# Attention and feed-forward block in float32 halves: probabilities times values by batch in four matmuls of 256 columns, later copies of the values, an earlier first mixing

## The chip, the cores and the metric

The kernel runs on one core of one Trainium2 chip. The metric is the device time of one execution in microseconds; lower is better. Of the kernel before there are three runs and one profiled execution.

## What is computed

32 batches of 64 tokens of width 1024, one transformer block. Cut to what matters:

```python
W = weights[condition]                                  # one 64x64 of 16, by batch
xm = einsum('bct,bcd->bdt', x, W)                       # the mixing: within a batch, over its 64 tokens
q, k, v = heads of xm @ Wq.T, xm @ Wk.T, xm @ Wv.T      # 32 query heads, 8 key heads, head width 128
q, k = rmsnorm(q) * q_norm_w, rmsnorm(k) * k_norm_w
attn = softmax(q @ k.T / sqrt(128) + bias)              # alibi slopes and causal mask, 64 x 64 by batch and head
x = x + (attn @ v) @ Wo.T
base = x @ weight.T + bias + scale * ((x @ a_sel.T) @ b_sel.T)        # a low-rank adapter, by batch
x = x + base @ W_base.T + b_base + 0.5 * (sum over 3 experts of irfft of decoded encodings)
```

All of it is float32. The feed-forward weights are folded into one matrix on the chip first.

## The kernel before

**Precision.** Every float32 operand of a matmul is kept as two halves that TensorE reads at full pace: hi, a copy rounded by ScalarE (`copy`, line 1226), and lo, what is left of it, a subtraction on VectorE (`low`, line 1480). A product of two such operands is three matmuls: hi by hi, hi by lo, lo by hi (`products`, line 1019). Weights come by DMA into four raw buffers (SyncE's queue), and w_hi and w_lo make a chunk in a ring of six slots.

**Order.** The whole order of the program is written out by a planner class, `Order`. Time in it is counted in quarters: a quarter is the products of one chunk, six matmuls of 512 columns. Each engine executes its own stages in the order of one common list, and waits for semaphores of the others. The table AT gives the due time of each stage in quarters after the products of its step; LATE is added for the last query step of a block; a stage is put at the first quarter that reaches its due time.

**Blocks.** Four blocks of 512 tokens, each of four tiles of 128 tokens, so two batches per tile. A block has key-value units (kv) and query units (q), each of four steps, one per tile; output units (o and p), which multiply the heads with Wo by a scheme of seven products; and two feed-forward units (f). In a block the order is kv, q, q, kv, o, q, q, kv, o, q, q, kv, o, q, q, p, o, f, f.

**A query step.** Four quarters of products give 128 tokens by 4 heads in one of four main banks. Then: square (ScalarE), mean (VectorE), rstd (GpSimd), scale (VectorE, which also empties the bank), query_t (TensorE transposes, line 1180), q_hi and q_lo, score (lines 1196 and 1197), alibied, biased and peak (VectorE), exp (ScalarE, line 1385), total, inverse and prob (VectorE), prob_t (TensorE transposes, line 1204), p_hi (ScalarE, line 1395), p_lo (VectorE, line 1681), pv (TensorE, line 1215), heads (ScalarE). A kv step has the same norm for its two key heads, gain (VectorE), key_t, k_hi, k_lo, and copies its two value heads as v_hi (ScalarE, straight after the products) and v_lo (VectorE).

**The product with the values.** Values have the tokens of both batches of a tile on the partitions. pt_hi and pt_lo hold the transposed probabilities of batch 0 in rows 0 to 63 of their first 256 columns and those of batch 1 in rows 64 to 127 of the other 256; the rest is zero from the start. So three matmuls of 512 columns give both batches:

```python
for m, (a, p) in enumerate(((v_hi, pt_hi), (v_hi, pt_lo), (v_lo, pt_hi))):
    mm = eng.matmul(pv_bank[...], a[:, t, g % 2, :], p[...], start=m == 0, stop=m == 2)
```

**Setup and the first mixing.** The setup folds the feed-forward weights: product(n, u) for n = 0 to 8 and u = 0, 1 is 24 matmuls (5.4 us) each; n = 8 stands for the adapter's b. Results leave by f_copy (ScalarE) and f_store (GpSimd's queue) through acc, so that x2 and x3, which load tiles 2 and 3 of x into the same place, wait for all f_store. A mixing of a tile is split_mix (x_hi, x_lo) and mix: four banks, each with four matmuls (lines 1103 and 1105), a_hi (ScalarE), a_rest and a_lo (VectorE, lines 1480 and 1483). `prepare(both=True)` loads and splits one weight chunk. "Rounds" (sums_load, sums_add t1 to t4, sums_store) form sums of parts of Wo on VectorE and GpSimd's queue; their due times are ROUND_AT.

**biased_x** (GpSimd, line 1848) adds a bias to a tile of acc, which VectorE's acc of unit f waits for. It is emitted with each tile's transposes of x1 (`transpose_x1`), which wait for the earlier tile's a_lo in the same banks.

Of the kernel before, what the change touches and what calls it, by code (L numbers as in the profile page):

```python
# [16 lines left out]
P = 128  # L17
# [25 lines left out]
AT = dict(square=0.15, mean=1.3, scale=1.7,  # L43
          tq=2.8, tq_hi=3.4, tq_lo=3.9,
          s=4.8, s_add=5.5, s_exp=6.3, s_norm=6.4,
          tp=7.9, tp_hi=8, tp_lo=8.6,
          v=10, v_hi=10.7, v_lo=11.3,
# [5 lines left out]
LATE = dict(s=0.5, s_add=0.5, s_exp=0.5, s_norm=0.5, tp=1.1, tp_hi=1.1, tp_lo=1.1, v=2.1, v_hi=2.1)  # L53
# [28 lines left out]
ROUND_AT = (0.5, 17, 33.5, 104, 180)  # L82
# [105 lines left out]
class Order(Plan):  # L188
# [34 lines left out]
    def setup(self):  # L223
# [55 lines left out]
        for n in range(KT):  # L279
# [17 lines left out]
            if n == 6:  # L297
                self.sums_load(*ROUNDS[2])
            self.product(n, 1)
# [138 lines left out]
    def blocks(self):  # L438
# [74 lines left out]
    def kv_step(self, k):  # L513
        self.wide(k, ("scale", (k,)))
        self.tick()
        base = self.quarter
        self.add("v_hi", k)

        def after_scale():
            self.add("gain", k)  # L520
            self.at(base, AT["tq"], transpose)
# [5 lines left out]
        self.norm(k, lambda: self.add("v_lo", k), after_scale)  # L527

    def norm(self, k, after_mean, after_scale):
# [3 lines left out]
        def mean():  # L533
            self.add("mean", k)
            self.add("rstd", k)
            after_mean()
# [4 lines left out]
        self.later(AT["square"], lambda: self.add("square", k))  # L541
# [3 lines left out]
    def q_step(self, k, g, t):  # L545
# [32 lines left out]
        def transpose_p():  # L578
            self.fill("pt", "prob_t", (k,), "p_lo")
            self.at(base, when("tp_hi"), lambda: self.add("p_hi", k))  # L580
            self.at(base, when("tp_lo"), lambda: self.add("p_lo", k))
# [13 lines left out]
        self.norm(k, lambda: None, after_scale)  # L595
# [58 lines left out]
    def transpose_x1(self, blk, t):  # L654
# [4 lines left out]
        self.add("biased_x", blk, t)  # L659
# [46 lines left out]
def build_program(nc, d, out):  # L706
# [3 lines left out]
    with ctx:  # L710
# [35 lines left out]
        v_hi = sb("v_hi", [P, TILES, 2, HD], F32R)  # L746
        v_lo = sb("v_lo", [P, TILES, 2, HD], F32R)
# [6 lines left out]
        prob = sb("prob", [P, 256])  # L754

# [45 lines left out]
        enc_rows = [v_hi[:, :, :, :].rearrange("p a b n -> p (a b n)"), v_lo[:, :, :, :].rearrange("p a b n -> p (a b n)")]  # L801
# [95 lines left out]
        def tile_of(k):  # L897
            return step(k)[3]
# [1053 lines left out]
```

## Time and profile before

| | |
|---|---|
| median of 3 runs | 2399.7 us (2398.89 to 2400.05) |
| the profiled execution | 2400.53 us, its span 2398.7 us |
| TensorE busy | 2368.9 us (99%), 11578 matmuls |
| VectorE busy | 1750.3 us (73%) |
| ScalarE busy | 1330.4 us (55%) |
| GpSimd busy | 280.5 us (12%) |
| matmuls of probabilities and values | 3 x 128, of 512 columns |

The span runs from the first to the last instruction; the execution's own time has some 2 us around it. Matmuls are pipelined, so that the time from one's start to the next's start counts, not its duration.

### The profile page before, as it was taken

To read this page: it belongs to the slowest core of one execution; us is meant where nothing else is said; L and a number is where in the kernel's file an instruction comes from. 1 tells how busy PE (TensorE), PEld (TensorE's weight loads), DVE (VectorE), ACT (ScalarE), POOL (GpSimd) and SP (SyncE) were. 2 spreads that over 40 slices of the span, in tenths; PEclk is the share of its full clock that TensorE was granted. 3 is DMA by queue.
4 is the path that set the end of the run, shared out by engine and by line. 5 is a ranking of instruction groups with operands and counts; after the bars stand their busy time and mean duration, and the time that the engine had idled before them with its cause. 6 is when DMAs were issued, how large, how long until landed. Compare 5 with 4: busy or idle time off the path is not lost.

```text
span 2398.7 us, 32788 instructions
## 1 busy us (share of the span) xinstructions
PE 2368.9 (99%) x11578; PEld 1967.4 (82%) x11578; DVE 1750.3 (73%) x2866; ACT 1330.4 (55%) x3305; POOL 280.5 (12%) x336
## 2 busy tenths in 40 slices
PE   8989999999999999999999999999999999999998
PEld 6878888888888888888888888888888888888886
DVE  6768878686847867777856777777876686868682
ACT  4246656566625656566724656565744565657560
POOL 0222010101111001010011101010011101010110
PEclk9999999999999999999999999999999999999999
DMA  7765434441542242423343242423244242424250
GB/s 258 257 256 199 154 134 148 140 149 63 188 145 92 88 139 76 141 79 129 134 156 118 71 158 71 158 71 123 97 170 148 77 147 69 153 77 141 70 194 35
DMA packets 88436, 316.12 MB, mean 132 GB/s; under 512 B 12716, under 2 KB 13228, under 8 KB 87124
## 3 DMA queue, kind: packets, MB, share of 16 engines
q1 hardware_dynamic: 70292, 247.14, 30.5%
q0 software_dynamic: 16256, 62.92, 7.2%
q10 hardware_dynamic: 1728, 3.98, 0.5%
q8 instruction: 94, 1.54, 0.3%
q14 instruction: 66, 0.54, 0.1%
HBM read 282.54 MB, written 31.46 MB: 131 GB/s over the span
## 4 chain that ended last, share of the span: by engine, by line
PE 94%; DVE 4%; issue 1%; DMA 1%; ACT 0%; POOL 0%; ACTq 0%; POOLq 0%; DVEq 0%
PE main L1019 79%; PE pv_bank L1215 4%; PE qt_bank L1180 3%; PE s_bank L1196 2%; PE s_bank L1197 2%; PE pt_bank L1204 1%; PE pt_bank L1019 1%; DVE ring L1480 1%; DVE act_lo L1480 0%; DVE act_lo L1483 0%; DVE setup L1480 0%; PE qt_bank L1117 0%; PE s_bank L1117 0%; DMA mask<-in_masks 0%; DMA t_scratch<-sums 0%
## 5 line engine op out<-in xcount | busy, mean ns | idle before, releaser
L1019 PE MATMUL main<-ring,act_hi 128*128 128x512 f32 x3584 | 1149.2, 402 | 0.1
L1019 PEld LDWEIGHTS main<-ring,act_hi 128*128 128x128 f32 x3584 | 641.3, 189 | 112.7 <-issue 2.1
L1019 PE MATMUL main<-ring,act_lo 128*128 128x512 f32 x1792 | 702.5, 392 | 0.0
L1019 PE MATMUL main<-ring,lefts 128*128 128x512 f32 x2688 | 624.3, 391 | 0.0
L1480 DVE TENSOR_TENSOR ring<-raw,ring 128x1024 fp32r<-128x1024 f32 x448 | 554.4, 1240 | 59.5 <-ACT ring L1226 58.0
L1019 PEld LDWEIGHTS main<-ring,lefts 128*128 128x128 f32 x2688 | 501.7, 188 | 103.0
L1226 ACT ACTIVATE ring<-raw 128x1024 fp32r<-128x1024 f32 x448 | 472.5, 1057 | 180.8 <-PE main L1019 163.6
L1019 PEld LDWEIGHTS main<-ring,act_lo 128*128 128x128 f32 x1792 | 336.8, 188 | 74.6
L1816 POOL TENSOR_TENSOR rstd<-mean,half 128x4 f32<-128x4 f32 (+1 forms) x192 | 174.7, 910 | 1568.5 <-DVE mean L1605 1568.3
L1385 ACT ACTIVATE prob<-score,peak 128x64 f32<-128x64 f32 x512 | 136.7, 338 | 157.3 <-DVE peak L1660 156.8
L1357 ACT ACTIVATE sq<-main 128x128 f32<-128x128 f32 x640 | 168.8, 277 | 70.7 <-PE main L1019 68.4
L1483 DVE TENSOR_TENSOR acc<-main,acc 128x512 f32<-128x512 f32 x164 | 112.2, 685 | 88.7 <-PE main L1019 88.4
L1681 DVE TENSOR_TENSOR pt_lo<-pt_bank,pt_hi 64x256 fp32r<-64x256 f32 x256 | 107.9, 421 | 72.8 <-ACT pt_hi L1395 71.1
L1395 ACT ACTIVATE pt_hi<-pt_bank 64x256 fp32r<-64x256 f32 x256 | 97.0, 379 | 112.4 <-PE pt_bank L1204 110.6
L1480 DVE TENSOR_TENSOR lefts<-quads,lefts 128x1024 fp32r<-128x1024 f32 x112 | 136.7, 1220 | 9.8 <-ACT lefts L1226 7.7
L1622 DVE TENSOR_TENSOR qn<-main,rstd 128x512 f32<-128x512 f32 (+1 forms) x192 | 114.3, 596 | 36.7 <-POOL rstd L1816 36.7
L1226 ACT ACTIVATE qt_hi<-qt_bank 128x512 fp32r<-128x512 f32 x128 | 76.7, 599 | 107.3 <-PE qt_bank L1180 102.3
L1226 ACT ACTIVATE lefts<-quads 128x1024 fp32r<-128x1024 f32 x112 | 118.7, 1060 | 29.9 <-PE main L1019 27.8
L1480 DVE TENSOR_TENSOR qt_lo<-qt_bank,qt_hi 128x512 fp32r<-128x512 f32 x128 | 87.9, 687 | 64.7 <-ACT qt_hi L1226 64.7
L1357 ACT ACTIVATION_READ_ACCUMULATOR sq<-main 128x1 f32 x640 | 132.8, 207 | 0.0
L1197 PE MATMUL s_bank<-k_t,qt_lo 128*128 128x64 f32 x512 | 117.2, 245 | 0.0
L1196 PE MATMUL s_bank<-k_t,qt_hi 128*128 128x128 f32 x512 | 114.6, 285 | 0.2
(172 smaller groups left out, 2390.4 us busy)
## 6 DMA issues: line engine op xcount, KB each, us to landing
raw<-in_wq SPq DMA_DIRECT2D x128, 512.0 KB, 4.0
raw<-t_scratch SPq DMA_DIRECT2D x128, 512.0 KB, 3.3
raw<-in_wo SPq DMA_DIRECT2D x96, 512.0 KB, 3.3
raw<-in_wkv SPq DMA_DIRECT2D x64, 512.0 KB, 4.1
sums<-in_wo POOLq DMA_DIRECT2D x32, 512.0 KB, 6.6
t_scratch<-sums POOLq DMA_DIRECT2D x32, 512.0 KB, 4.2
raw<-f_scratch SPq DMA_DIRECT2D x32, 512.0 KB, 5.5
acc<-in_x POOLq DMA_DIRECT2D x16, 512.0 KB, 3.7
```

Of the source, the lines that this page charges most:

```text
L1019: mm = eng.matmul(bank, a, b, start=start and n == 0 and m == 0, stop=stop and n == len(terms) - 1 and m == 2, skip_group_check=further)
L1196: eng.matmul(s_bank[:, a:a + 2 * SEQ], lh, keys, start=True, stop=False)
L1197: mm = eng.matmul(s_bank[:, a:a + SEQ], ll, keys[:, 0:SEQ], start=False, stop=True)
L1226: eng.activation(dst, src, ACT.Copy).then_inc(done[stage], 1)
L1357: act = eng.activation(sq[:, tile(h)], norm_bank(k)[:, tile(h)], ACT.Square, accum_out=ssum[:, h:h + 1])
L1385: act = eng.activation(prob[:, cols], score[:, cols], ACT.Exp, bias=peak[:, r:r + 1], scale=-1.0)
L1395: act = eng.activation(pt_hi[rows_of(b), b, :], pt_bank[rows_of(b), 0:256], ACT.Copy)
L1480: eng.tensor_tensor(dst, src, f32(upper), ALU.subtract).then_inc(done[stage], 1)
L1483: eng.tensor_tensor(dst, a, b, ALU.add).then_inc(done[stage], 1)
L1622: eng.tensor_tensor(heads_of(norm_tile(k)[:, cols], heads), heads_of(norm_bank(k)[:, cols], heads), along(rstd[:, 0:heads], heads), ALU.mu ...
L1681: rest = eng.tensor_tensor(pt_lo[rows_of(b), b, :], pt_bank[rows_of(b), 0:256], f32(pt_hi[rows_of(b), b, :]), ALU.subtract)
L1816: eng.tensor_tensor(rstd[:, 0:heads], mean[:, 0:heads], half[:, 0:heads], ALU.pow).then_inc(done[stage], 1)
```

## The change

1. The values of a tile are kept by batch: `values[:, t, g, b, :]` has v_hi of batch b in the batch's own half of the partitions and v_lo of the same batch in the other half. pt_hi has the hi probabilities of a batch in both halves: a new stage p_twice (ScalarE) copies each from one half into the other. One matmul with `values` and pt_hi so gives v_hi by p_hi plus v_lo by p_hi, and one with pt_lo gives v_hi by p_lo: two matmuls of 256 columns for each batch.
2. v_hi is two copies of 64 rows, and waits for scale (due at 1.9 instead of straight after the products); v_lo is two subtractions that write the other half (due 2.3, behind gain).
3. Due times: p_twice 9.2, pv 10.6 (10 before), heads 11.5 (10.7); LATE 1.2 and 1.6 (1.1 and 2.1).
4. The first mixing: tiles 0 and 1 are mixed before product(7, 1) and product(8, 0); x_hi and x_lo of tile 2 stand before product(8, 0); tile 2 is mixed after chunk 4; tile 3 is split before the first kv step and mixed before the second.
5. The rounds of the sums come 2 to 4 quarters later.
6. biased_x is emitted for two tiles together, and waits for the later one's a_lo.

```diff
-          tp=7.9, tp_hi=8, tp_lo=8.6,
-          v=10, v_hi=10.7, v_lo=11.3,
+          tp=7.9, tp_hi=8, tp_again=9.2, tp_lo=8.6,
+          v=10.6, v_hi=11.5,
...
-ROUND_AT = (0.5, 17, 33.5, 104, 180)
+ROUND_AT = (4.5, 20, 35.5, 104, 180)
...
+            if n == KT - 1:
+                self.mix(0, 0)
             self.product(n, 1)
...
+        self.mix(0, 1)
+        self.split_mix(0, 2)
         self.product(KT, 0)
+        for i in range(UNIT_CHUNKS):
+            self.prepare(both=True)
+        self.product(KT, 1)
         self.prepare(both=True)
-        self.mix(0, 0)
+        self.mix(0, 2)
         self.prepare(both=True)
-        self.prepare(both=True)
-        self.split_mix(0, 2)
-        self.prepare(both=True)
+        self.split_mix(0, 3)
         self.load(("lora_a",), ("loraa_lo", ()))
         self.add("loraa_hi")
         self.add("loraa_lo")
-        self.product(KT, 1)
-        self.mix(0, 1)
-        self.prepare(both=True)
-        self.prepare(both=True)
         self.add("fx_store")
...
-            if k == 0:
-                self.split_mix(0, 3)
-            if k in (1, 2):
-                self.mix(0, k + 1)
+            if k == 1:
+                self.mix(0, 3)
...
-        self.add("biased_x", blk, t)
+        if t % 2 == 1:
+            for half in (t - 1, t):
+                self.add("biased_x", blk, half)
...
-        v_hi = sb("v_hi", [P, TILES, 2, HD], F32R)
-        v_lo = sb("v_lo", [P, TILES, 2, HD], F32R)
+        values = sb("values", [P, TILES, 2, BPT, HD], F32R)
...
-                    w.wait_ge("p_hi", k)
+                    w.wait_ge("p_twice", k)
...
-                    for m, (a, p) in enumerate(((v_hi, pt_hi), (v_hi, pt_lo), (v_lo, pt_hi))):
-                        mm = eng.matmul(pv_bank[:, :, :].rearrange("p b n -> p (b n)"), a[:, t, g % 2, :],
-                                        p[:, :, :].rearrange("p b n -> p (b n)"), start=m == 0, stop=m == 2)
+                    for b in range(BPT):
+                        both = values[:, t, g % 2, b, :]
+                        eng.matmul(pv_bank[:, b, :], both, pt_hi[:, b, :], start=True, stop=False)
+                        mm = eng.matmul(pv_bank[:, b, :], both, pt_lo[:, b, :], start=False, stop=True)
...
+                elif stage == "p_twice":
+                    k, = key
+                    w.wait_ge("p_hi", k)
+                    for b in range(BPT):
+                        act = eng.activation(pt_hi[rows_of(1 - b), b, :], f32(pt_hi[rows_of(b), b, :]), ACT.Copy)
+                    act.then_inc(done["p_twice"], 1)
...
                 elif stage == "v_lo":
                     k, = key
                     w.wait_ge("square", k)
-                    low(v_lo[:, tile_of(k), :, :], norm_bank(k)[:, 2 * HD:4 * HD].rearrange("p (j n) -> p j n", j=2),
-                        v_hi[:, tile_of(k), :, :], stage, k)
+                    w.wait_ge("v_hi", k)
+                    for b in range(BPT):
+                        rest = eng.tensor_tensor(values[rows_of(1 - b), tile_of(k), :, b, :], values_in(k, b),
+                                                 f32(values[rows_of(b), tile_of(k), :, b, :]), ALU.subtract)
+                    rest.then_inc(done[stage], 1)
```

How this moves the stages, at three places. The first is TensorE's list at the product of probabilities and values in a query unit (qt_bank is the transposes of the queries, main a quarter of products). Before:

```order
L1215 MATMUL pv_bank<-pt_hi,v_hi 128x512
L1215 MATMUL pv_bank<-pt_lo,v_hi 128x512
L1215 MATMUL pv_bank<-pt_hi,v_lo 128x512
L1019 MATMUL main<-ring,act_hi 128x512 x2
L1019 MATMUL main<-ring,act_lo 128x512
L1019 MATMUL main<-ring,act_hi 128x512 x2
L1019 MATMUL main<-ring,act_lo 128x512
L1180 MATMUL qt_bank<-ident,qn_75 128x128 x4
```

Now:

```order
L1027 MATMUL main<-ring,act_hi 128x512 x2
L1027 MATMUL main<-ring,act_lo 128x512
L1027 MATMUL main<-ring,act_hi 128x512 x2
L1027 MATMUL main<-ring,act_lo 128x512
L1224 MATMUL pv_bank<-pt_hi,values 128x256
L1225 MATMUL pv_bank<-pt_lo,values 128x256
L1224 MATMUL pv_bank<-pt_hi,values 128x256
L1225 MATMUL pv_bank<-pt_lo,values 128x256
L1188 MATMUL qt_bank<-ident,qn_75 128x128 x4
```

The product stands one quarter later, directly ahead of the query transposes.

The second place is ScalarE's list where a query unit's last softmax meets the first step of a kv unit (v_hi and now values are the copies of the values, sq the squares, prob the exp of the last query step). Before:

```order
L1395 ACTIVATE pt_hi<-pt_bank 64x256 x2
L1226 ACTIVATE v_hi<-main 128x256
L1357 ACTIVATE sq,ssum<-main 128x128 x2
L1385 ACTIVATE prob<-score,peak 128x64 x4
L1226 ACTIVATE quads<-pv_bank 128x2x4x64
```

Now:

```order
L1406 ACTIVATE pt_hi<-pt_bank 64x256 x2
L1368 ACTIVATE sq,ssum<-main 128x128 x2
L1412 ACTIVATE pt_hi<-pt_hi 64x256 x2
L1360 ACTIVATE values<-main 64x2x128 x2
L1396 ACTIVATE prob<-score,peak 128x64 x4
```

The copies of the values, which now wait for VectorE's scale, stand directly ahead of the exp.

The third place is VectorE's list at the end of the setup, (ring is w_lo of a chunk, act_lo a piece of a mixing, x_odd x_lo of tile 3, lefts x_lo of tile 2, extra the adapter's parts). Before:

```order
L1483 TENSOR_TENSOR act_lo<-pv_bank,act_lo 128x2x128
L1480 TENSOR_TENSOR ring<-raw_69,ring 128x1024
L1480 TENSOR_TENSOR ring<-raw_70,ring 128x1024
L1480 TENSOR_TENSOR x_odd<-acc,x_odd 128x1024
L1480 TENSOR_TENSOR act_lo<-qt_bank,act_hi 128x2x128
```

Now:

```order
L1497 TENSOR_TENSOR ring<-raw_68,ring 128x1024
L1497 TENSOR_TENSOR act_lo<-qt_bank,act_hi 128x2x128
L1500 TENSOR_TENSOR act_lo<-qt_bank,act_lo 128x2x128
L1497 TENSOR_TENSOR act_lo<-s_bank,act_hi 128x2x128
L1500 TENSOR_TENSOR act_lo<-s_bank,act_lo 128x2x128
L1497 TENSOR_TENSOR act_lo<-pt_bank,act_hi 128x2x128
L1500 TENSOR_TENSOR act_lo<-pt_bank,act_lo 128x2x128
L1497 TENSOR_TENSOR act_lo<-pv_bank,act_hi 128x2x128
L1500 TENSOR_TENSOR act_lo<-pv_bank,act_lo 128x2x128
L1497 TENSOR_TENSOR ring<-raw_69,ring 128x1024
L1497 TENSOR_TENSOR x_odd<-acc,x_odd 128x1024
L1497 TENSOR_TENSOR extra<-raw_70,extra 128x1024
```

The split of tile 3 stands behind both w_lo and the mixing of tile 2 as before, but TensorE's mixing of tile 3, which needs it, has moved from the third kv step to the second.

## Rows read from the trace of the kernel before

**Rows 1.** The page: busy us (share of the span) x instructions, by engine.

```profile
PE 2368.9 (99%) x11578; PEld 1967.4 (82%) x11578; DVE 1750.3 (73%) x2866; ACT 1330.4 (55%) x3305; POOL 280.5 (12%) x336
```

**Rows 2.** The page: the chain that ended last, by engine.

```profile
PE 94%; DVE 4%; issue 1%; DMA 1%; ACT 0%; POOL 0%; ACTq 0%; POOLq 0%; DVEq 0%
```

**Rows 3.** Waits of TensorE: engine line <- releaser: us, times, longest.

```profile
PE qt_bank L1180 <- DVE qn L1629: 5.3, 3, 3.5
...
PE qt_bank L1117 <- DVE act_lo L1480: 2.4, 1, 2.4
PE qt_bank L1103 <- DVE act_lo L1483: 1.9, 2, 1.0
```

**Rows 4.** Behind the longest wait: busy PE, PEld, DVE, ACT, POOL; PEclk.

```profile
155.00:159.00 4.00, 3.63 (x12) 3.06 (x13) 1.87 (x3) 0.77 (x2) 0.00 (x0) 0.57 0.05 19
```

**Rows 5.** Chain in order of time, block 1: start, us, what.

```profile
881.78 0.22 PE pt_bank L1204 x2
...
885.65 0.68 PE pv_bank L1215 x3
886.34 1.36 PE main L1019 x6
```

**Rows 6.** The same view after the wait of 2.4 us.

```profile
660.33 6.41 PE main L1019 x21
```

**Rows 7.** Low-rank stage: the chain, then line 1019's loads, min/median/max.

```profile
666.74 2.87 PE pt_bank L1019 x24
...
L1019 PEld LDWEIGHTS pt_bank<-act_hi,extra x16: 187/192/192, 649.8 to 652.7; 128*128 128x128 f32 x16
```

**Rows 8.** ScalarE in order of time, one query step.

```profile
224.85 0.77 ACT L1395 ACTIVATE pt_hi<-pt_bank 64x256 fp32r<-64x256 f32 x2 [1.01 <-PE pt_bank L1204]
...
226.66 1.07 ACT L1226 ACTIVATE ring<-raw 128x1024 fp32r<-128x1024 f32 x1
```

**Rows 9.** From query to key steps: ScalarE, VectorE, TensorE in order of time.

```profile
244.52 1.07 ACT L1385 ACTIVATE prob<-score,peak 128x64 f32<-128x64 f32 x4 [1.93 <-DVE peak L1660]
...
244.40 0.41 DVE L1622 TENSOR_TENSOR qn<-main,rstd 128x256 f32<-128x256 f32 x1
...
246.29 0.43 DVE L1675 TENSOR_TENSOR prob<-prob,inv 128x256 f32<-128x256 f32 x1
...
248.02 0.38 PE L1204 MATMUL pt_bank<-ident,prob 128*128 128x128 f32 x2
```

**Rows 10.** All engines at 654 us in order of time.

```profile
654.06 2.68 POOL L1848 TENSOR_TENSOR acc<-acc,bias_eff 128x1024 f32<-128x1024 f32 x1 [4.07 <-PE s_bank L1117]
...
654.39 3.43 DVE L1480 TENSOR_TENSOR ring<-raw,ring 128x1024 fp32r<-128x1024 f32 x1
```

**Rows 11.** DMA issues at 125.25 and from 138: count, KB, us to landing.

```profile
acc<-in_x POOLq DMA_DIRECT2D x1, 512.0 KB, 7.4
...
raw<-in_wq SPq DMA_DIRECT2D x2, 512.0 KB, 5.9
```

**Rows 12.** VectorE in order of time at the first mixing.

```profile
143.12 0.69 DVE L1480 TENSOR_TENSOR extra<-main,extra 128x512 fp32r<-128x512 f32 x1
143.72 0.42 DVE L1480 TENSOR_TENSOR act_lo<-qt_bank,act_hi 128x256 fp32r<-128x256 f32 x1
...
149.14 1.22 DVE L1480 TENSOR_TENSOR x_odd<-acc,x_odd 128x1024 fp32r<-128x1024 f32 x1
```

**Rows 13.** TensorE at the end of product 8.

```profile
133.78 0.39 PE L1019 MATMUL main<-setup,act_lo 128*128 128x512 f32 x1
```

**Rows 14.** TensorE in the mixing of tile 3.

```profile
159.03 0.33 PE L1103 MATMUL s_bank<-mixw,x_odd 128*128 128x256 f32 x1
159.20 0.22 PE L1105 MATMUL s_bank<-mixw,x_odd 128*128 128x128 f32 x1
159.25 0.34 PE L1103 MATMUL s_bank<-mixw,x_odd 128*128 128x256 f32 x1
...
160.41 0.45 PE L1019 MATMUL main<-ring,act_hi 128*128 128x512 f32 x1
```

More of the change, by code:

```diff
@@ L40 @@
 SCALING = 16.0 / 32.0
-AT = dict(square=0.15, mean=1.3, scale=1.7,
+AT = dict(square=0.15, mean=1.3, scale=1.7, values=1.9, values_lo=2.3,
           tq=2.8, tq_hi=3.4, tq_lo=3.9,
           s=4.8, s_add=5.5, s_exp=6.3, s_norm=6.4,
-          tp=7.9, tp_hi=8, tp_lo=8.6,
-          v=10, v_hi=10.7, v_lo=11.3,
+          tp=7.9, tp_hi=8, tp_again=9.2, tp_lo=8.6,
+          v=10.6, v_hi=11.5,
           add=1.6,
@@ L51 @@
           w_hi=0.3, w_lo=0.9)
-LATE = dict(s=0.5, s_add=0.5, s_exp=0.5, s_norm=0.5, tp=1.1, tp_hi=1.1, tp_lo=1.1, v=2.1, v_hi=2.1)
+LATE = dict(s=0.5, s_add=0.5, s_exp=0.5, s_norm=0.5, tp=1.2, tp_hi=1.2, tp_again=1.2, tp_lo=1.2, v=1.6, v_hi=1.6)
 OPS = (("11", "11", "a"), ("s3", "t3", "d"), ("12", "21", "a"), ("s2", "t2", "b"),
@@ L513, in kv_step @@
     def kv_step(self, k):
-        self.wide(k, ("scale", (k,)))
+        self.wide(k, ("v_lo", (k,)))
         self.tick()
         base = self.quarter
-        self.add("v_hi", k)
+        self.later(AT["square"], lambda: self.add("square", k))
         def after_scale():
             self.add("gain", k)
+            self.at(base, AT["values"], lambda: self.add("v_hi", k))
+            self.at(base, AT["values_lo"], lambda: self.add("v_lo", k))
             self.at(base, AT["tq"], transpose)
@@ L526, in transpose, with norm @@
             self.at(base, AT["tq_lo"], lambda: self.add("k_lo", k))
-        self.norm(k, lambda: self.add("v_lo", k), after_scale)
-    def norm(self, k, after_mean, after_scale):
+        self.norm(k, after_scale)
+    def norm(self, k, after_scale):
         self.norm_no[k] = len(self.norms)
@@ L535, in mean @@
             self.add("rstd", k)
-            after_mean()
         def scale():
@@ L580, in transpose_p @@
             self.at(base, when("tp_hi"), lambda: self.add("p_hi", k))
+            self.at(base, when("tp_again"), lambda: self.add("p_twice", k))
             self.at(base, when("tp_lo"), lambda: self.add("p_lo", k))
@@ L594, in after_scale @@
                 self.at(base, when(name), work)
-        self.norm(k, lambda: None, after_scale)
+        self.later(AT["square"], lambda: self.add("square", k))
+        self.norm(k, after_scale)
     def o_step(self, k, blk, pair, m):
@@ L799, in build_program @@
         bias_parts = k_flat.rearrange("p (u s n) -> p u s n", u=2, s=2)
-        enc_rows = [v_hi[:, :, :, :].rearrange("p a b n -> p (a b n)"), v_lo[:, :, :, :].rearrange("p a b n -> p (a b n)")]
-        enc_hi = v_hi[0:ENC, :, :, :].rearrange("p a b n -> p (a b n)")
-        enc_lo = v_lo[0:ENC, :, :, :].rearrange("p a b n -> p (a b n)")
+        v_flat = values[:, :, :, :, :].rearrange("p t g b n -> p (t g b n)")
+        enc_rows = [v_flat[:, 0:CHUNK], v_flat[:, CHUNK:2 * CHUNK]]
+        enc_hi, enc_lo = (part[0:ENC, :] for part in enc_rows)
         x_even = [lefts[:, 2, i, :, :, :].rearrange("p a h n -> p (a h n)") for i in range(2)]
@@ L1344, in _ @@
                     k, = key
-                    w.wait_ge("mm", k, 3)
+                    w.wait_ge("scale", k)
                     if last_heads(k) is not None:
@@ L1349, in _ @@
                         w.wait_ge("weff_mm", KT, 1, 3)
-                    copy(v_hi[:, tile_of(k), :, :], norm_bank(k)[:, 2 * HD:4 * HD].rearrange("p (j n) -> p j n", j=2), "v_hi")
+                    for b in range(BPT):
+                        act = eng.activation(values[rows_of(b), tile_of(k), :, b, :], values_in(k, b), ACT.Copy)
+                    act.then_inc(done["v_hi"], 1)
                 elif stage == "square":
@@ L1608, in _ @@
                     w.wait_ge("square", k)
-                    low(v_lo[:, tile_of(k), :, :], norm_bank(k)[:, 2 * HD:4 * HD].rearrange("p (j n) -> p j n", j=2),
-                        v_hi[:, tile_of(k), :, :], stage, k)
+                    w.wait_ge("v_hi", k)
+                    for b in range(BPT):
+                        rest = eng.tensor_tensor(values[rows_of(1 - b), tile_of(k), :, b, :], values_in(k, b),
+                                                 f32(values[rows_of(b), tile_of(k), :, b, :]), ALU.subtract)
+                    rest.then_inc(done[stage], 1)
                 elif stage == "scale":
```

5 lines of the change are left out of this document (3 added, 2 removed).

## The prediction

> **What bounds the kernel now.** Read the busy shares first: TensorE is busy for 2368.9 us, 99% of the span, VectorE for 73%, ScalarE for 55%, GpSimd for 12% [rows 1]. The chain that ended last is 94% TensorE and 4% VectorE [rows 2]. So the kernel's time is its list of matmuls at their pace, plus a few stalls: a cut in the matmuls is worth its full time, work added to the other engines is worth nothing while TensorE waits for none of it. The waits of TensorE are next [rows 3]: outside the start and the setup's beginning they are 5.3 us for transposes of keys and queries that wait for VectorE's gain (3.5 in one piece), 1.9 for mixing banks, 2.4 for the transposes of x1. A long wait has a tail: after the one of 3.5 us the granted clock of the next 4 us is 0.57 of full, which is the lower level, 1.2 GHz, for most of it [rows 4]; after the one of 2.4 us, 21 matmuls that take 4.8 us elsewhere (0.227 each, by six in 1.36) take 6.41 [rows 5, 6]. A wait over 2 us thus costs some 1.6 us on top.
>
> **Part 1, the products of probabilities and values.** There are 128 (one for each query step). Each is now three matmuls of 512 columns, 0.68 us from its first to the next stage's first [rows 5]. Afterwards it is four of 256. The trace has matmuls of this very shape (128x128 stationary, 256 moving columns, each with its own weight load) in the low-rank stage: 24 in 2.87 us, 0.1196 each [rows 7]. Four are 0.478 us, so one step saves 0.20 us, and 128 save **25.8 us**. Both ends: if columns alone counted, a matmul of half the columns would take half of 0.227, four of them 0.454, a saving of 29 us. The other end is weight loads that don't hide: one lasts 0.187 to 0.192 [rows 7], four are 0.76 us, a loss of 0.08 a step, 10 us in all. I take the 0.1196, since it is the same instruction with the same weight load.
> The Trainium skill (TensorE: Matmul & The Clock Gate, Back-to-back issue gap) gives N/2.4 + 2.5 ns between matmuls at the full clock: 216 ns for 512 columns, 109 for 256. By it, called an estimate, the group would go from 0.65 to 0.44 us and the 128 would save 27 us. The rows show 227 and 120, some 10 ns more each, and I go by them.
>
> **Part 2, what the four matmuls need.** pt_hi must hold each batch's probabilities in both halves of the partitions, so ScalarE gets two more copies a step (p_twice), 64x256 from SBUF to SBUF. The nearest row is p_hi, two of 64x256 from PSUM in 0.77 us [rows 8]; a copy from SBUF of four times the columns takes 1.07. I take 0.8 us a step, 102 us in all. v_hi becomes two copies of 0.38 for one of 0.384 (64 steps, +24 us). ScalarE goes from 55% to about 61%. VectorE's v_lo becomes two of 0.42 for one (+27 us of 1750). None of it lies on TensorE's list; it costs only where the cover is gone. The cover: now the transposes of the probabilities end at 882.0 and the product starts at 885.65, 3.6 us later [rows 5]. The product's due time goes from 10 to 10.6, which by the order is one quarter (six matmuls, 1.36 us) later, so the window is 5.0 us. In it ScalarE has p_hi (0.77), the next square and, in the worst steps, a ring copy (1.07), all done 2.9 us after p_hi's start [rows 8], then p_twice: 3.7. Over 1 us is left. The exp of the next step, which waits for VectorE, stands behind p_twice. So I cost it at 0.
> v_hi is moved behind scale, and is so ahead of exp where a query unit's last softmax meets the first step of the next key unit (three times a block, 12 in all). There scale ends at 244.82, two copies take 0.76, exp then starts at 245.6 instead of 244.52, and VectorE's total, inverse and prob end at about 247.8 instead of 246.72, with the transposes due at 248.02 less the 0.2 us that the product gives back [rows 9]. The margin of 1.3 us shrinks to about nothing: 0 to 0.3 us each, 12 times; I take **+1 us**. The main bank of a key step is held until v_lo instead of scale, about 1 us of the 16 or more quarters before its next use: nothing.
>
> **Part 3, biased_x.** In block 0 the addition of the bias on GpSimd (2.68 us from 654.06) covers VectorE's w_lo, which lasts 3.43 us instead of 1.24 [rows 10]; behind it on VectorE's queue stand acc and the act_lo that the next transposes of x1 wait for. This is the wait of 2.4 us [rows 3], with 1.6 us of half clock behind it [rows 6]. Now biased_x runs after both tiles' act_lo, so nothing of it runs at 654: w_lo ends 2.2 us earlier and the stall and its tail go, all but 0.2: **-3.8 us**. What it collides with next: two additions back to back (4.9 us) after the second pair, against a w_lo whose chunk is for a later unit, and VectorE has nothing due there. The other three blocks have no such wait, and stay.
>
> **Part 4, the first mixing.** Mixing of tiles 0 and 1 goes ahead, into the products with w2, where VectorE is idle. That takes sixteen pieces of 0.42 off VectorE's queue there, and its two waits (1.9 us) go. But follow the rest. The mixing of tile 0 (1.8 us) stands ahead of the product whose store x2's load waits for, so that x2 and x3 are issued 1.6 us later; x2's load, issued at 125.25, takes 7.4 us [rows 11] and will land at 134.3. On ScalarE x_hi of tile 2 now stands ahead of all six weight copies: it ends at 135.4, x_lo at 136.6, beff_lo 0.7 and w_lo of chunk 0 (1.24) bring 138.5. Chunk 4 is loaded into the buffer that this frees: 5.9 us as the two loads issued there now [rows 11], 144.4. On ScalarE its copy stands ahead of the mixing pieces of tile 2 (1.06, 145.5); on VectorE w_lo (146.7), eight act_lo of 0.42 (150.0), w_lo of chunk 5 (151.3), x_lo of tile 3 (152.5) [rows 12]. TensorE ends product 8 at 133.9 today [rows 13] and 1.8 later now, at 135.8, waits 0.8 for x_lo of tile 2, mixes it, does key step 0, and is at the mixing of tile 3 at 144.0, which needs that last x_lo: **a wait of 8.5 us**, in place of those of 0.8 (mixing), 3.5 (keys) and others. Then mixing, key step 1 and 1.6 us of low clock end at 161.6; today the same work ends at 160.4 [rows 14]. So +1.2 us there. After that, today's small waits for keys and queries (1.1, 0.6, 0.3 and less) partly go, as gain stands ahead of v_lo, and the sums' rounds, 2 to 4 quarters later, bring one or two others: 0. I take **+1 us**. Bounds: all of the 9 us of waits and low clock there go (5.3, 1.9 and 1.6), -9; the rounds' collisions come on top, +7.
>
> **Sum.** -25.8 + 1 - 3.8 + 1 = -27.6 us against the profiled execution's 2400.5 us, 2372.9; the median of the runs is 0.8 below that execution, so 2372.
>
> **Rivals.**
> A: the product doesn't get the pace of the low-rank stage. In the mixing, a matmul of 256 columns starts 0.17 us before the next one [rows 14], and at four times 0.17 the new product costs the old 0.68. Against it: there the next is one of 128 columns that starts 0.05 later, and the pair takes 0.23, 0.115 each. If weight loads don't hide at all the product takes 0.76, +10 us, and the whole comes to 2400.5 + 10 + 1 - 3.8 + 1 = 2409, slower than before; it decides from 0.17 us a matmul. Chance 3%.
> B: ScalarE is late with p_twice. From 0.2 us of wait a product the saving is gone, from 0.25 (for example 1.3 us more queue than counted, at each step) the kernel is slower. The order speaks against it; in one step of five it would give 26 waits of some 0.3 us, 2380. With the 12 places of part 2 at 0.3 and a second one like them, 2382. Chance 10%.
> C: part 4 goes as its cover suggests: x2 lands earlier since fewer transfers compete, the wait at tile 3 is 0 to 3 us and has no tail: -6 to -9 instead of +1, 2363. For it: the loads of those 20 us differ among themselves, 7.4 and 5.9 us for the same size [rows 11], so the queue before them counts for much. Chance 15%.
> D: the edit does nothing that shows. Excluded but for A: 512 columns fewer a step stand in the order.
>
> **How the numbers follow.** My own case, parts 1 to 4 as summed, has 72%, and its own range is 2366 to 2380: 3 us for part 1's pace (112 to 125 ns), 4 for part 4. With B and C the range is 2362 to 2383. 0.2% is 4.8 us, about what a measurement of this kernel can tell from no change. Faster by more than that: all of my case, B and C but for a tail, 0.94. Within it 0.03 (B at its worst, A at 0.165). Slower 0.03 (A).
>
> **What would show it.** Right: four matmuls of the product at some 0.12 us from start to start; TensorE's busy time down by some 26 us; no waits of TensorE for pt_hi; no w_lo of over 3 us near 654; TensorE's longest wait the mixing of tile 3 near 144, 8 us, with a low clock behind it. Wrong: starts 0.17 apart (A); waits on pv_bank for ScalarE (B); the mixing of tile 3 without a wait (C); several waits of the probabilities' transposes for VectorE at the changes from query to key units (part 2).

## The result, and the profile after

| | before | after |
|---|---|---|
| median | 2399.88 us (4 runs, 2398.89 to 2400.09) | 2434.95 us (4 runs, 2433.82 to 2436.59) |
| ratio | | 1.0144, 95% interval 1.0132 to 1.0156 |
| span of the profiled execution | 2398.7 us | 2433.0 us |

The changed kernel is 35 us slower. The forecast was 28 us faster, 2372 in a range of 2362 to 2383: wrong, in sign too.

The page of the changed kernel, its busy shares and its chain, which answer to [rows 1, 2]:

```profile
PE 2365.7 (97%) x11706; PEld 1970.9 (81%) x11706; DVE 1784.7 (73%) x2930; ACT 1464.8 (60%) x3625; POOL 296.4 (12%) x336
...
PE 84%; DVE 9%; issue 2%; ACT 1%; DMA 1%; POOL 1%; DVEq 0%; ACTq 0%; POOLq 0%
```

TensorE's busy time is only 3 us less than before, and the span is 34 us longer: TensorE waits more, and works part of the time at the lower clock, where a matmul counts as busy for longer. VectorE's share of the chain has gone from 4% to 9%. What TensorE waits for is in the waits of the changed kernel, against [rows 3] (what waited, for what, us in total, times, the longest):

```profile
PE qt_bank L1188 <- DVE qn L1649: 30.3, 25, 2.2
PE qt_bank L1111 <- DVE x_odd L1497: 9.4, 1, 9.4
PE pv_bank L1058 <- ACT pt_lo L1266: 4.6, 1, 4.6
PE qt_bank L1188 <- DVE qn L1642: 3.5, 3, 1.9
PE s_bank L1204 <- issue: 1.9, 4, 1.1
```

The second row is the mixing of tile 3, which part 4 put at 8.5 us. The first is what the forecast missed: transposes of keys (L1188) that wait for gain (L1649), 30.3 us in 25 places, where it was 5.3 in 3.

**An account by places.** Both kernels do the same 192 transposes of keys and queries in the same order. The start of each after the change, less its start before, is a running difference; where it steps, time is lost or won. From the two traces:

| place | us |
|---|---|
| the start, up to the first key step behind query units (246.42 before, 255.41 after) | +9.0 |
| transposes of the fourth key step of a unit with an o unit behind it: 12 places, 2.12 each | +25.4 |
| transposes of the second and third: 12 places, 0.25 and 0.28 | +6.4 |
| the o unit behind the fourth: 8 of the 12 places, 1.6 each | +12.9 |
| end of block 0, start of block 1 | -4.2 |
| starts of blocks 1 to 3 | +1.2 |
| all else: the products, less small waits | -16.2 |
| **sum, at the last transpose** | **+34.5** |

Three rows, 44.7 us, belong to one pattern. The timeline of the kernel before at the first of the twelve places, VectorE from the third key step's transposes (258.96) to the fourth's (264.72), with GpSimd's rstd between its rows (start, duration, engine, line, operation; in brackets the idle time before it):

```profile
257.77 1.22 DVE L1480 TENSOR_TENSOR ring<-raw,ring 128x1024 fp32r<-128x1024 f32 x1
258.90 1.22 DVE L1480 TENSOR_TENSOR lefts<-quads,lefts 128x1024 fp32r<-128x1024 f32 x1
260.04 0.41 DVE L1480 TENSOR_TENSOR k_t<-qt_bank,k_t 128x256 fp32r<-128x256 f32 x1
260.37 1.21 DVE L1480 TENSOR_TENSOR ring<-raw,ring 128x1024 fp32r<-128x1024 f32 x1
261.70 0.17 DVE L1605 TENSOR_SCALAR mean<-ssum 128x2 f32<-128x2 f32 x1
261.78 0.42 DVE L1480 TENSOR_TENSOR v_lo<-main,v_hi 128x256 fp32r<-128x256 f32 x1
...
261.95 0.70 POOL L1816 TENSOR_TENSOR rstd<-mean,half 128x2 f32<-128x2 f32 x1 [5.02 <-DVE mean L1605]
...
262.65 1.23 DVE L1480 TENSOR_TENSOR ring<-raw,ring 128x1024 fp32r<-128x1024 f32 x1 [0.45 <-ACT ring L1226]
263.79 0.42 DVE L1622 TENSOR_TENSOR qn<-main,rstd 128x256 f32<-128x256 f32 x1
264.24 0.42 DVE L1629 TENSOR_TENSOR qn<-qn,kgain 128x256 f32<-128x256 f32 x1
```

The same of the changed kernel, from the third's transposes (268.46) to the fourth's:

```profile
268.78 0.86 DVE L1628 TENSOR_TENSOR values<-main,values 64x256 fp32r<-64x256 f32 x2 [0.38 <-ACT values L1360]
269.67 1.22 DVE L1497 TENSOR_TENSOR ring<-raw,ring 128x1024 fp32r<-128x1024 f32 x1
270.81 1.22 DVE L1497 TENSOR_TENSOR lefts<-quads,lefts 128x1024 fp32r<-128x1024 f32 x1
272.06 0.42 DVE L1497 TENSOR_TENSOR k_t<-qt_bank,k_t 128x256 fp32r<-128x256 f32 x1
272.40 1.22 DVE L1497 TENSOR_TENSOR ring<-raw,ring 128x1024 fp32r<-128x1024 f32 x1
273.53 0.16 DVE L1622 TENSOR_SCALAR mean<-ssum 128x2 f32<-128x2 f32 x1
273.60 1.22 DVE L1497 TENSOR_TENSOR ring<-raw,ring 128x1024 fp32r<-128x1024 f32 x1
...
273.77 1.60 POOL L1836 TENSOR_TENSOR rstd<-mean,half 128x2 f32<-128x2 f32 x1 [6.29 <-DVE mean L1622]
...
275.41 0.42 DVE L1642 TENSOR_TENSOR qn<-main,rstd 128x256 f32<-128x256 f32 x1 [0.59 <-POOL rstd L1836]
...
275.87 0.42 DVE L1649 TENSOR_TENSOR qn<-qn,kgain 128x256 f32<-128x256 f32 x1
...
276.35 0.44 PE L1188 MATMUL qt_bank<-ident,qn 128*128 128x128 f32 x2 [1.96 <-DVE qn L1649]
```

Before, v_lo stands between mean and scale, beside GpSimd's rstd, for which VectorE has to wait anyway: it is free. Now v_lo is two instructions behind gain, and waits 0.38 for v_hi, which starts only when scale has ended. That is 0.38 + 0.86 = 1.24 us more on VectorE's queue between gain and the next mean, at each key step, and here VectorE has the subtractions of ring, lefts, k_t and ring without a break. Mean of the fourth key step starts 2.74 us behind the third's transposes before (261.70 - 258.96) and 5.07 now (273.53 - 268.46): 2.33 more, of which 1.24 comes from this step and the rest from the step ahead of it, which used up a slack of 1.1 us (gain ended at 257.85 before, for transposes at 258.96). From mean to scale it takes 2.09 before and 1.88 now, 0.21 less. 2.33 - 0.21 = 2.12, the step in the table.

In 8 of the 12 places the o unit behind it works at the lower clock for most of 4 us. The changed kernel by stretches behind the second stall (401.9), and behind the first (276.4), which is one of the four places without (us, then busy time and count of PE, PEld, DVE, ACT and POOL, then the granted clock, where 0.50 is 1.2 GHz throughout, the DMA share and GB/s):

```profile
276.40:278.40 2.00, 2.00 (x10) 1.69 (x11) 1.69 (x3) 1.98 (x5) 0.00 (x0) 1.00 0.82 262
401.90:403.90 2.00, 1.91 (x6) 1.63 (x7) 1.58 (x4) 1.98 (x4) 0.00 (x0) 0.58 0.81 256
403.90:405.90 2.00, 2.00 (x6) 1.50 (x6) 1.97 (x3) 0.96 (x2) 0.00 (x0) 0.56 0.11 43
```

**The product itself** did what part 1 said. In the timeline of a query step of the changed kernel:

```profile
334.09 0.28 PE L1224 MATMUL pv_bank<-pt_hi,values 128*128 128x256 f32 x1
334.20 0.28 PE L1225 MATMUL pv_bank<-pt_lo,values 128*128 128x256 f32 x1
334.32 0.28 PE L1224 MATMUL pv_bank<-pt_hi,values 128*128 128x256 f32 x1
334.44 0.29 PE L1225 MATMUL pv_bank<-pt_lo,values 128*128 128x256 f32 x1
334.56 0.60 PE L1188 MATMUL qt_bank<-ident,qn 128*128 128x128 f32 x4
```

Four matmuls in 0.47 us (median of all 128 is 0.475), where three took 0.68 [rows 5].

### The profile page after: what moved, and what is told of

Its sections match the earlier page's. It is cut to its first block, busy times and chain, and to the rows that moved or that the text cites. A ratio compares the mean times of both kernels' runs of the same rounds, so it can differ in the third digit from the quotient of the medians.

```text
span 2433.0 us, 33487 instructions
## 1 busy us (share of the span) xinstructions
PE 2365.7 (97%) x11706; PEld 1970.9 (81%) x11706; DVE 1784.7 (73%) x2930; ACT 1464.8 (60%) x3625; POOL 296.4 (12%) x336
## 4 chain that ended last, share of the span: by engine, by line
PE 84%; DVE 9%; issue 2%; ACT 1%; DMA 1%; POOL 1%; DVEq 0%; ACTq 0%; POOLq 0%
PE main L1027 71%; PE qt_bank L1188 3%; PE s_bank L1204 3%; PE s_bank L1205 2%; DVE ring L1497 1%; DVE lefts L1497 1%; POOL rstd L1836 1%; PE pt_bank L1212 1%; PE pv_bank L1225 1%; PE pv_bank L1224 1%; PE pt_bank L1027 1%; DVE qn L1642 1%; DVE quads L1708 1%; ACT values L1360 1%; DMA acc<-in_x 1%
## 5 line engine op out<-in xcount | busy, mean ns | idle before, releaser
L1027 PE MATMUL main<-ring,lefts 128*128 128x512 f32 x2688 | 637.3, 396 | 0.0
L1027 PEld LDWEIGHTS main<-ring,lefts 128*128 128x128 f32 x2688 | 509.9, 191 | 105.7
L1836 POOL TENSOR_TENSOR rstd<-mean,half 128x4 f32<-128x4 f32 (+1 forms) x192 | 185.5, 966 | 1584.0 <-DVE mean L1622 1579.0
L1188 PE MATMUL qt_bank<-ident,qn 128*128 128x128 f32 x640 | 105.4, 279 | 35.2 <-DVE qn L1649 30.3
L1188 PEld LDWEIGHTS qt_bank<-ident,qn 128*128 128x128 f32 x640 | 73.6, 140 | 58.9 <-DVE qn L1649 44.7
```

The costliest lines, as they stand in the source:

```text
L1027: mm = eng.matmul(bank, a, b, start=start and n == 0 and m == 0, stop=stop and n == len(terms) - 1 and m == 2, skip_group_check=further)
L1188: mm = eng.transpose(qt_bank[:, tile(h)], norm_tile(k)[:, tile(h)], ident[:, :])
L1836: eng.tensor_tensor(rstd[:, 0:heads], mean[:, 0:heads], half[:, 0:heads], ALU.pow).then_inc(done[stage], 1)
```

## The experiments

Theories. **1:** v_lo has left the shadow of rstd; VectorE's queue makes the key transposes late. **2:** ScalarE's added load (p_twice, doubled copies) does. **3:** the first mixing and the rounds shifted the whole stream. Every ratio is to the kernel before, run beside it on the same chip.

### Values early again

```
-        self.wide(k, ("v_lo", (k,)))
+        self.wide(k, ("scale", (k,)))
+        self.add("v_hi", k)
...
-            self.at(base, AT["values"], lambda: self.add("v_hi", k))
-            self.at(base, AT["values_lo"], lambda: self.add("v_lo", k))
...
             self.add("mean", k)
             self.add("rstd", k)
+            after_mean()
```

> The changed kernel with the values copied early again: v_hi (two copies) right behind the key step's products and ahead of its square, v_lo (two) between mean and scale, the main bank given back at scale; the four matmuls of 256 columns, p_twice, biased_x and the first mixing stay as changed. Theory 1 (VectorE's queue): where v_lo stood between mean and scale it lay beside GpSimd's rstd (0.70 us) and cost VectorE's queue nothing; behind gain it adds its own 0.86 us and a wait of 0.38 for v_hi to every key step, mean of the fourth key step before an o unit comes 1.9 us late, and a ring subtraction beside rstd makes that last 1.60 instead of 0.70. By it the 12 places of 2.12 + 0.25 + 0.28 us and the 8 tails of 1.6 us of low clock go, 44.7 us: 2390, between 2383 and 2396. Theory 2 (ScalarE's load): p_twice's 103 us are in the way; then nothing goes: 2430 to 2440. Theory 3 (the first mixing and the rounds moved the whole stream): 2430 to 2440 too.

Measured: 2406.0, ratio 1.0025 (1.0016 to 1.0035). 29 us come back: theory 1 has the cause, its number was too good by 16. The tails (the stretches of low clock) are gone, and the fourth transposes wait 0.68 instead of 1.96, yet they still wait, and the starts of blocks 1 to 3 cost some 4.5 us more than in the changed kernel. The timeline at the first of the twelve places shows why: v_lo is now two instructions, and a ring subtraction still follows it, ahead of scale.

```profile
268.14 0.17 DVE L1622 TENSOR_SCALAR mean<-ssum 128x2 f32<-128x2 f32 x1
268.34 0.86 DVE L1628 TENSOR_TENSOR values<-main,values 64x256 fp32r<-64x256 f32 x2
...
268.39 0.70 POOL L1836 TENSOR_TENSOR rstd<-mean,half 128x2 f32<-128x2 f32 x1 [5.01 <-DVE mean L1622]
...
269.23 1.23 DVE L1497 TENSOR_TENSOR ring<-raw,ring 128x1024 fp32r<-128x1024 f32 x1
270.49 0.42 DVE L1642 TENSOR_TENSOR qn<-main,rstd 128x256 f32<-128x256 f32 x1
```

Mean to scale is 2.35 us against 2.09, and mean itself is 0.52 later behind the third transposes than before (the doubled v_hi stands ahead of square on ScalarE): together 0.78 a place.

### The move of the values alone, on the kernel before

```
-        self.wide(k, ("scale", (k,)))
+        self.wide(k, ("v_lo", (k,)))
...
+            self.at(base, AT["values"], lambda: self.add("v_hi", k))
+            self.at(base, AT["values_lo"], lambda: self.add("v_lo", k))
```

> The kernel before with one part of the change alone: v_hi (one copy of 0.39 us) behind scale and v_lo (one of 0.42) behind it, in the places the change gives them, the bank given back at v_lo; three matmuls of 512 columns, no p_twice, mixing and biased_x as before. Theory 1: VectorE's queue gets 0.39 + 0.42 = 0.8 us per key step instead of 1.24, but the ring subtraction stands beside rstd all the same: 12 stalls of 0.8 to 2.1 us, some with 1.6 us behind them: 2412 to 2440, likeliest 2425. Theories 2 and 3: the same as before, 2400 within 3 us.

Measured: 2409.3, ratio 1.0037 (1.0023 to 1.0052): 9 us slower, with three matmuls and without p_twice. The likeliest value of theory 1 was 16 too high, and the measurement is just outside its range; theories 2 and 3 fall as sole causes. The waits of the key transposes for gain, 5.3 us in 3 places before, are

```profile
PE qt_bank L1181 <- DVE qn L1631: 10.8, 15, 2.1
```

The 12 places are there, at 0.70 us each with no tail, and in each of them rstd lasts 1.60, at the first of them:

```profile
264.35 1.60 POOL L1818 TENSOR_TENSOR rstd<-mean,half 128x2 f32<-128x2 f32 x1 [5.22 <-DVE mean L1606]
```

The 0.8 us that the move adds to VectorE's queue behind the second key step is covered by the slack of 1.1, so that the third's transposes are not late, and only what the third step adds shows at the fourth. So the move alone costs 0.70 a place, and the doubling alone (the kernel with early values above) 0.78 at the fourth step and 0.26 at the second. Both together cost 2.12, 0.25 and 0.28, and mostly a tail. That is more than their sum, since the slack can be used only once.

### The first mixing and rounds as before, and the rounds alone

```
-ROUND_AT = (4.5, 20, 35.5, 104, 180)
+ROUND_AT = (0.5, 17, 33.5, 104, 180)
```

The first of these two kernels has this line and the old order of the mixing of tiles 0 to 3 (mix(0, 0) and mix(0, 1) behind the products of n = 8, and so on as before the change); the second has this line alone.

> The changed kernel with the first mixing and the rounds' places (ROUND_AT) of the kernel before. Theories 1 and 2: only the start changes: the wait of 9.4 us goes and those of 3.5, 1.9 and 1.1 us and a tail of 1.6 come back: 2424 to 2433. Theory 3: the regular stalls go too: 2375 to 2400.

> The changed kernel with the rounds' places (ROUND_AT) of the kernel before, the first mixing as changed. In the changed kernel GpSimd's rstd of the first query step stands behind four loads of the sums' next round, each of which waits for a store to land (185.2 to 188.2), and the query transposes come 1.9 us late, with low clock behind. Theory R (the rounds' places cost most of the 7.4 us at the start): 2428 to 2431. Theory M (the mixing's place costs them): 2433 to 2436.

Measured: 2427.7, ratio 1.0115 (1.0099 to 1.0132), with both; 2428.1, ratio 1.0124 (1.0108 to 1.0139), with the rounds alone. The regular stalls stay in both (here with the rounds alone), so theory 3 falls for them:

```profile
PE qt_bank L1188 <- DVE qn L1649: 29.2, 26, 2.0
```

Both medians are 7 us below the changed kernel's, inside what was expected (theory R for the rounds alone). But the intervals of the ratios meet the changed kernel's, 1.0132 to 1.0156, so the places in the traces have to decide. The first key step behind query units starts at 255.41 in the changed kernel, 249.73 with the old rounds and 247.90 with both. So 5.7 of the 9.0 us at the start are the rounds' places, and 1.8 are the mixing's new place, which the two medians can't tell from nothing. These shares are not a sum: early values alone shorten the start too.

One mechanism of the rounds shows in GpSimd's timeline of the changed kernel:

```profile
185.20 0.53 POOL L1849 DMA_DIRECT2D sums<-in_wo  x1 [2.56 <-DMA t_scratch<-sums]
187.70 0.53 POOL L1849 DMA_DIRECT2D sums<-in_wo  x1 [1.97 <-DMA t_scratch<-sums]
188.25 1.04 POOL L1836 TENSOR_TENSOR rstd<-mean,half 128x4 f32<-128x4 f32 x1
```

The loads of the next round wait on GpSimd's queue until a store has landed, and rstd of the first query step, whose mean was there since 185.46, stands behind them.

### Scale and gain of key steps in mean's quarter

The changed kernel with kv_scale at 1.35, where scale is at 1.7:

```
-        self.later(AT["scale"], scale)
+        self.later(AT["kv_scale" if self.units[self.steps[k][0]][0] == "kv" else "scale"], scale)
```

> The changed kernel with scale and gain of key steps due in the same quarter as mean, so that the ring subtraction (and in some places the three of the softmax) stands behind gain instead of between mean and scale; values stay late. Theory 1: rstd lasts 0.70 in the 12 places instead of 1.60 and scale doesn't wait for 1.22 us of subtraction, so the stall shrinks from 1.96 us to about 1 and has no tail: 2435 - 12 x 0.9 - 13 = 2411, between 2403 and 2420. If the queue and the overlap with rstd are not what holds the key transposes: 2430 to 2440.

Measured: 2411.8, ratio 1.0045 (1.0028 to 1.0062), on the number. At the first place:

```profile
271.66 0.16 DVE L1622 TENSOR_SCALAR mean<-ssum 128x2 f32<-128x2 f32 x1
...
271.90 0.70 POOL L1836 TENSOR_TENSOR rstd<-mean,half 128x2 f32<-128x2 f32 x1 [6.29 <-DVE mean L1622]
...
272.63 0.42 DVE L1642 TENSOR_TENSOR qn<-main,rstd 128x256 f32<-128x256 f32 x1 [0.81 <-POOL rstd L1836]
```

Mean to scale is 0.97 instead of 1.88, which is the whole of the 0.90 us that each of the 12 places gives back; the eight tails go too. Mean is as late as in the changed kernel (5.08 behind the third transposes), so the late mean and the long way from mean to scale are separate terms.

### Without p_twice, and with single copies

Both start from the kernel with early values.

```
-            self.at(base, when("tp_again"), lambda: self.add("p_twice", k))
```

> The changed kernel with early values, less p_twice: ScalarE's two further copies of the probabilities are left out, so the product of their rounded part with the values' remainder is not computed. Theory 1 (VectorE's queue holds the key transposes, ScalarE's added load does not): the same as with early values and p_twice, 2406, between 2402 and 2407. Theory 2 (ScalarE's load counts: v_hi, square and with them mean come later behind p_twice): the waits of 0.7 and 0.4 us at the key transposes that are left shrink by half or more, 2392 to 2400.

Measured: 2403.1, ratio 1.0011 (1.0002 to 1.0021), 2.9 us less than with p_twice. ScalarE's busy time goes from 1466.3 to 1358.2 us, and the waits of key transposes for gain stay:

```profile
PE qt_bank L1187 <- DVE qn L1648: 16.7, 28, 1.9
```

They were 16.8 in 28 with p_twice. Theory 2 falls; 108 us of work on ScalarE cost some 3. The intervals of the two kernels just overlap (this one's ends at 1.0021, the other's begins at 1.0016), but the traces agree with the medians: the first key transposes of block 3 start at 1845.71 here and at 1848.83 with p_twice.

```
-                    for b in range(BPT):
-                        act = eng.activation(values[rows_of(b), tile_of(k), :, b, :], values_in(k, b), ACT.Copy)
+                    act = eng.activation(values[:, tile_of(k), :, 0, :], full, ACT.Copy)
```

and v_lo likewise.

> The changed kernel with early values, v_hi and v_lo each done as one instruction over 128 partitions instead of two over 64: the four matmuls of the product, p_twice and all else run as they are, but the values' parts don't stand where the product needs them, so the products are not the reference's. Theory 1: one 128-partition instruction lasts as long as one over 64 (0.39 and 0.42 us), so the path from products to key transposes is 0.38 shorter, VectorE's queue 0.43; the 12 places of 0.78 + 0.27 and the 3 further ones at the starts of blocks go: 2406 - 12.6 - 2 = 2391, between 2387 and 2397. Theory 2 (p_twice delays them): 2400 to 2406.

Measured: 2388.6, ratio 0.9949 (0.9932 to 0.9966): theory 1, 2 us beyond its likeliest. The waits for gain are down from 16.8 us in 28 places to 4.3 in 13, and at the 12 places there is none:

```profile
PE qt_bank L1188 <- DVE qn L1649: 4.3, 13, 1.0
```

The doubling of v_hi and v_lo accounts for the 12 places that early values had left, and more: 17 us.

### biased_x in its old place

```
-        if t % 2 == 1:
-            for half in (t - 1, t):
-                self.add("biased_x", blk, half)
+        self.add("biased_x", blk, t)
```

> The changed kernel with biased_x in its old place (an addition behind each tile's transposes). If part 3 was right, block 0 gets back its ring subtraction of over 3 us beside GpSimd's addition near 665 and the wait of 2.4 us with its tail: 2435 + 3.8 = 2439, between 2437 and 2441. If the pair of additions costs as much elsewhere (in blocks 1 to 3 of the changed kernel a ring subtraction of 3.4 us begins beside the first of a pair): 2433 to 2436.

Measured: 2438.9, ratio 1.0163 (1.0146 to 1.018). The median is 3.9 us over the changed kernel's, but these four runs lie between 2435.0 and 2441.8 and the two intervals overlap (the changed kernel's is 1.0132 to 1.0156), so the medians alone don't show it. The place does: from the last query transposes of block 0 to the first key transposes of block 1 this kernel takes 3.65 us longer than the changed one, and from there on, low clock aside, the two stay within 0.4 us of each other. The wait came back with its cause, in that kernel's waits and timeline:

```profile
PE qt_bank L1123 <- DVE act_lo L1495: 2.4, 1, 2.4
```

```profile
668.17 2.68 POOL L1866 TENSOR_TENSOR acc<-acc,bias_eff 128x1024 f32<-128x1024 f32 x1 [4.09 <-PE s_bank L1123]
...
668.50 3.44 DVE L1495 TENSOR_TENSOR ring<-raw,ring 128x1024 fp32r<-128x1024 f32 x1
```

### Put together

Early values, new biased_x, mixing and rounds of the kernel before; first with scale in mean's quarter at all key steps, then at the fourth of a unit only:

> Put together: the four matmuls of 256 columns, p_twice and the new biased_x, with early values, scale and gain of key steps in mean's quarter (v_lo still between mean and scale, the ring subtraction behind gain), and the first mixing and rounds of the kernel before. Theory 1: 2406 less 7.4 (the old start, as measured on the changed kernel) less 12 x 0.78 (no 1.22 us of subtraction between v_lo and scale) less about 2 at the starts of blocks: 2387, between 2381 and 2393, faster than before. Theory 2 (ScalarE's load): 2398 or more.

> As the put-together kernel (early values, old start, new biased_x), but scale and gain stand in mean's quarter only at the fourth key step of a unit. In the version before they stood so at all four, and at the first key step behind a query unit that put them ahead of the three softmax instructions: 12 waits of 0.7 us of the probabilities' transposes for prob (8.1 us in all). Theory 1: these go and nothing comes back, since the ring subtraction stood between mean and scale only at the fourth: 2394 - 8 - 1 = 2385, between 2381 and 2390. Other theory (what VectorE doesn't do there it does later, so that the 12 places lose their 0.7 us at the next key transposes): 2391 to 2395.

Measured: 2393.8, ratio 0.9973 (0.9963 to 0.9984), 1 us above its range; and 2385.1, ratio 0.9934 (0.992 to 0.9948), on the number. What was missing in the first is in its waits:

```profile
PE pt_bank L1213 <- DVE prob L1696: 8.1, 12, 0.7
```

Scale and gain had moved ahead of the three softmax instructions where a key unit follows a query unit, and exp, total and prob were late by them. Held back to the fourth step, all 8 us came.

The last one makes scale and gain of key steps one stage:

```
+                        for h in range(heads):
+                            one = eng.scalar_tensor_tensor(norm_tile(k)[:, tile(h)], norm_bank(k)[:, tile(h)], rstd[:, h:h + 1],
+                                                           kgain[:, :], ALU.mult, ALU.mult)
```

> The same, and scale and gain of a key step made one stage: two instructions of 128x128 (times rstd, times the gain) in place of two of 128x256. Theory 1: each 128x128 lasts some 0.27 us (estimate from 0.42 for 256 columns, half of it being columns), 0.54 + 0.03 in place of 0.88, so each key step's path and VectorE's queue get back 0.3 us of the 0.43 that the doubled v_lo takes; the waits of 0.35 us at the second key transposes and what is left at the others go: 3 to 6 us less than without it, 2380, between 2376 and 2386. Other theory (VectorE's queue has slack there by now): the same within 1.5 us.

Measured: 2378.0, ratio 0.9908 (0.9893 to 0.9923), the fastest: 22.5 us faster than before, 57 faster than the change. An instruction lasts 0.34 instead of the 0.27 estimated, but two lie over each other and take 0.61, against 0.88. In its timeline, the fourth key step:

```profile
260.94 0.17 DVE L1622 TENSOR_SCALAR mean<-ssum 128x2 f32<-128x2 f32 x1 [0.26 <-ACT sq L1368]
261.14 0.86 DVE L1628 TENSOR_TENSOR values<-main,values 64x256 fp32r<-64x256 f32 x2
262.03 0.61 DVE L1645 SCALAR_TENSOR_TENSOR qn<-main,rstd,kgain 128x128 f32<-128x128 f32 x2
```

VectorE has a gap again ahead of mean, and of waits of key transposes one in the setup is left (3.3 us).

## Why the prediction was wrong, point by point

**Part 1 was right.** It had 0.478 us a product, from the low-rank stage; 0.475 was measured. Of 26 us, some 3 are lost again at the transposes that now stand right behind the product: in 26 of the 128 places these begin some 0.1 us late.

**Part 2 is the step that failed**, and with it the sign. It forecast +1 us; the table has 44.7, and the late values take more at the start (early values alone make the start 3.3 us shorter, 5.67 against 8.99 at the first key step behind query units). Of this 29 us go with early values and another 17 with single copies. "VectorE's v_lo becomes two of 0.42 for one (+27 us of 1750). None of it lies on TensorE's list; it costs only where the cover is gone" was the right question, and the text then asked it of p_twice, and of exp where query units end, but not of v_lo. V_lo's cover was the wait for rstd, and the edit itself took v_lo out of it. The text never opened VectorE's queue at the end of key units: there VectorE has the subtractions of ring, lefts, k_t and ring back to back, and TensorE has a slack of 1.1 us. An average (VectorE 73% busy) stood for a stretch where it was nearly full (5.45 of the 6.02 us from 257.77 to 263.79). A second term was missing too: without v_lo the ring subtraction starts beside rstd, which then lasts 1.60 instead of 0.70. The 12 places named, with 0 to 0.3 us at the probabilities' transposes, did not show a wait; the 12 that cost are four key steps later.

P_twice was right at nearly nothing: some 3 us, for 108 us on ScalarE. The bank held until v_lo made no wait.

**Part 3 was right:** -3.8 forecast, 3.65 at its place when it is taken back.

**Part 4 was right in its place and wrong in its sum.** The wait at the mixing of tile 3 is 9.4 us, for x_odd's subtraction, where 8.5 was forecast; the key transposes behind it are 2.7 us later than before, where 1.2 was. "The sums' rounds, 2 to 4 quarters later, bring one or two others: 0" is the second step that failed: 5.7 us at the start, as the kernel with the old rounds shows, near the upper bound of 7 that the text itself had given and set aside. Its "a wait over 2 us thus costs some 1.6 us on top" rested on two waits, of 2.4 and 3.5 us; here the same 1.6 followed waits of 1.96 and 1.98 in 8 places of 12.

The rivals: A (pace) false. B had a late ScalarE and a price of 0.2 us a product; false. C false. The one on the slower side was A with 3%; the mechanism that decided had no chance at all, since no rival was drawn from the wait that the edit adds.

Left open: how the 0.91 us between mean and scale in the changed kernel splits between the 1.22 us of subtraction in the queue and the rstd that lasts 0.90 longer beside it. By the rows the subtraction alone would have ended at 274.82 and scale started then instead of at 275.41, so 0.59 would be rstd's; no run separates them. What decides which of the 12 stalls of 1.96 us have a low clock behind them is open too.

## What to carry to other kernels

An instruction that stands in another engine's round trip (here between mean and scale) is free. Moved out, it adds its whole length to its own queue, and that costs what exceeds the slack there: 0.8 us more per step cost 0.70 a place, 1.24 more cost 2.65 and mostly a tail. So look for such places before moving anything, and cost a moved instruction on its own queue in the fullest stretch, not by the engine's average. Splitting an instruction over 128 partitions into two over 64 doubled its time here: v_lo went from 0.42 to 0.86 us and v_hi from 0.38 to 0.77. Where a layout needs that, pay for it by merging neighbours on the same queue, as scale and gain were.

## What the runs showed of the hardware

GpSimd's rstd (128x2) lasts 0.70 us alone or beside v_lo, and 1.60 beside a ring subtraction that had started first, in all 12 places, and in all 12 of the kernel before with the late values alone; it ends 0.55 after the subtraction does, in each of them. V_lo reads one operand from PSUM, the ring subtraction reads both from SBUF. With that the rows agree with the Trainium skill (SBUF — State Buffer, SBUF: two separate sides), which says that a VectorE instruction with two SBUF inputs and a GpSimd instruction that reads SBUF exclude each other for the whole of the one that started first. The addition of biased_x beside the subtraction, 3.44 instead of 1.22, is the same the other way round.

After a wait of 1.96 to 1.98 us TensorE's clock was at its lower level, 1.2 GHz, for most of 4 us in 8 of 12 places and not in 4; after one of 1.07, 0.68 or 0.6, in none of 12 each. The place in the program doesn't decide it: three other kernels with a wait of 1.96 to 2.00 us at the same 12 places (old mixing and rounds, old rounds alone, old biased_x) had it at 8, 6 and 7 of them, and not at the same ones. Each is worth 1.6 us; that two executions of one program can differ by as much for this reason is an estimate from these traces, since each kernel has one.

A wait costs TensorE 0.10 to 0.16 us more than its idle time: 1.96 us idle made 2.12, 1.07 made 1.22, and 0.68 made 0.78.
